# Second layer of a two-layer graph attention kernel: own rows loaded after their product, nine edge groups scaled by ScalarE, and the next exponent ahead of the activation

## The reference, cut to what matters

```
h = relu(layernorm(x));  x = x + attention0(h, input, adj, weight)
h = relu(layernorm(x)) @ W
e[m, n] = leaky_relu(h[m] . a_src + h[n] . a_dst)        where adj[m, n] > 0, else -1e9
att = softmax(e, axis=1);  att = where(att >= 1e-4, att, 0) * (valid entries of the row)
x = x + elu(h + att @ h)
```

## Time and profile before

| | |
|---|---|
| median of three runs | 630.43 us (630.30 to 631.12) |
| profiled execution | 629.07 us |
| its span, first to last instruction | 627.4 us |
| busy: TensorE, VectorE, ScalarE, GpSimd | 412.0, 462.9, 418.8, 300.1 us |
| VectorE's `take(1)` to `take(5)` start at | 551.06, 561.16, 572.24, 583.21, 594.18 us |
| last instruction of the second layer (VectorE) starts | 619.58 us |

### The profile page before, as it was taken

The page is one execution under the profiler, slowest core; times in us unless marked ns, Lnnn a source line. Parts: engine busy times, 40 slices in busy tenths (PEclk is TensorE's granted clock), DMA queues, the critical chain, the costliest instruction groups (busy, mean ns, idle before and its releaser), DMA issues.

```text
span 627.4 us, 9941 instructions
## 1 busy us (share of the span) xinstructions
PE 412.0 (66%) x3079; PEld 273.4 (44%) x3079; DVE 462.9 (74%) x2116; ACT 418.8 (67%) x460; POOL 300.1 (48%) x337
## 2 busy tenths in 40 slices
PE   2457476767877777786859677686756371268873
PEld 0112143443645455463635345363636361157653
DVE  0095268797979898997969799797986835279992
ACT  3567779889988989899879798988322030025451
POOL 6000851333315060607757563365777777777500
PEclk9655677997987979799969889799685675579998
DMA  8999999999999999999999999995122223235531
GB/s 322 414 419 422 419 405 408 409 406 412 403 414 380 370 401 392 403 388 404 396 402 384 395 387 399 390 376 188 53 69 64 60 74 103 54 71 154 141 103 54
DMA packets 37768, 186.80 MB, mean 298 GB/s; under 512 B 7888, under 2 KB 8144, under 8 KB 18896
## 3 DMA queue, kind: packets, MB, share of 16 engines
q1 hardware_dynamic: 28352, 166.75, 67.5%
q0 software_dynamic: 9216, 19.11, 10.6%
q10 hardware_dynamic: 144, 0.27, 0.1%
HBM read 179.73 MB, written 6.37 MB: 297 GB/s over the span
## 4 chain that ended last, share of the span: by engine, by line
DVE 36%; DMA 20%; ACT 12%; PE 11%; POOL 10%; issue 8%; SPq 2%; DVEq 0%; ACTq 0%
DMA arena<-in_adj 19%; ACT arena L892 8%; POOL arena L834 7%; PE K L1538 3%; DVE keys L1081 3%; POOL arena L826 2%; ACT R_all L921 2%; PE K L1783 2%; DVE G L1191 2%; DVE RTp L1485 1%; DVE RTp L1250 1%; DVE stats L1297 1%; ACT hx L901 1%; DVE cand L1110 1%; DVE cand L1098 1%
## 5 line engine op out<-in xcount | busy, mean ns | idle before, releaser
L892 ACT ACTIVATE arena<-arena,half_c 128x2048 fp8e4<-128x2048 int32 x144 | 284.2, 1999 | 45.5 <-DMA arena<-in_adj 40.2
L826 POOL DMA_INDIRECT X<-in_L_gnn_input,idx_all x132 | 125.4, 950 | 167.9 <-DVE idx_near L1162 130.4
L1538 PE MATMUL K<-arena,bits 128*128 128x512 fp8e4 x576 | 170.3, 436 | 16.8 <-ACT arena L892 16.7
L834 POOL DMA_INDIRECT arena<-table,idx_near x96 | 92.7, 965 | 36.8 <-issue 28.6
L1538 PEld LDWEIGHTS K<-arena,bits 128*128 128x128 bf16 x576 | 59.7, 109 | 91.0 <-ACT arena L892 25.9
L1081 DVE MAX8 keys<-K 128x8 int32<-128x128 f32 x192 | 42.4, 281 | 40.4 <-PE K L1538 40.3
L834 POOL DMA_INDIRECT E<-table,idx_near x48 | 46.0, 959 | 28.9 <-DMA table<-hs 14.5
L1536 PE MATMUL K<-key_add,key_one 128*128 128x512 bf16 x48 | 20.7, 430 | 45.2 <-ACT arena L892 23.4
L850 POOL TENSOR_TENSOR E<-E 128x3072 f32<-128x3072 f32 (+3 forms) x4 | 12.9, 3223 | 51.1 <-DMA E<-in_L_gnn_input 50.9
L1631 PE MATMUL W<-X,RTp 128*128 128x128 f32 x240 | 35.2, 285 | 1.2 <-ACT hs L937 0.8
L1550 PE MATMUL G<-g,R_all 128*128 128x128 bf16 x324 | 25.0, 226 | 16.1 <-DVE g L1213 13.5
(11 more groups left out here) (281 smaller groups left out, 962.2 us busy)
## 6 DMA issues: line engine op xcount, KB each, us to landing
arena<-in_adj SPq DMA_DIRECT2D x144, 1024.0 KB, 11.3
hs<-table SPq DMA_DIRECT2D x12, 262.0 KB, 2.8
E<-in_L_gnn_input SPq DMA_DIRECT2D x3, 1024.0 KB, 15.0
out_x<-x_all SPq DMA_DIRECT2D x12, 256.0 KB, 3.1
table<-hs SPq DMA_DIRECT2D x11, 262.0 KB, 7.8
x_all<-in_x SPq DMA_DIRECT2D x1, 2560.0 KB, 13.8
X<-in_L_gnn_input,idx_all POOLq DMA_INDIRECT x132, 5.6
arena<-table,idx_near POOLq DMA_INDIRECT x96, 2.7
```

The lines of the kernel that those rows point to most:

```text
L826: pool.indirect_dma_start(out=x_of(b)[:, e, :], out_offset=None, in_=inp, in_offset=bass.IndirectOffsetOnAxis(ap=idx_all[:, at:at + 1], ax ...
L834: pool.indirect_dma_start(out=E(g, t, 1)[:, 0, :], out_offset=None, in_=tables[g], in_offset=bass.IndirectOffsetOnAxis(ap=idx_near[:, t, g ...
L892: nc.scalar.activation(sign[:, load % SIGNS, :], ring[:, load % RING, :], ACT.Sign, bias=half_c[:], scale=1.0, saturate=False).then_inc(si ...
L1538: last = mm(bank_[:], bits[:, third * TB + j, :], sign[:, load % SIGNS, j * FOLD:(j + 1) * FOLD], start=False, stop=(third == G - 1 and j ...
```

## The change

Four edits, all in the second layer.

```
-    BY_ACT = 6
+    BY_ACT = 9
```

`own_r`, a new semaphore, is counted up by the matmul of `own_rows2(j)`, and SyncE waits for it in place of `att2_r`:

```
                 for j in range(T // B + 1):
                     if j + 2 < T // B:
-                        sp.wait_ge(att2_r, j + 1)
+                        sp.wait_ge(own_r, j + 1)
                         own(j + 2)
...
                     pe.wait_ge(h2_r[j % 2], 16 * sum(len(halves(k)) for k in range(j % 2, j + 1, 2)))
-                    mm(quads(att2[j % 4]), ident[:], h2[j % 2], start=True, stop=False)
+                    mm(quads(att2[j % 4]), ident[:], h2[j % 2], start=True, stop=False).then_inc(own_r, 1)
```

On ScalarE the exponent of group i comes before the odd block's activation:

```
                     if 0 <= i - 1 < NQ:
                         exponent2_of_edges(i - 1)
                         scale_last_edges(i - 1)
+                    if i < NQ:
+                        exponent2(i)
                     if 0 <= i - 2:
                         elu_parts(2 * (i - 2) + 1)
-                    if i < NQ:
-                        exponent2(i)
```

More of the change, by code:

```diff
@@ L625, in fast_path @@
         h2_r = [sem("h2_r0"), sem("h2_r1")]
-        take_early_r, take_r, rows2_r, cen2, ex2_r, pk_r, shares2_r, d2_r, exp2_e_r, RTp2_r, att2_r, src_r, neg_r, w_act_r, scaled_r, e_r, out_r, out_stored = (
-            sem(s) for s in ("take_early_r", "take_r", "rows2_r", "cen2", "ex2_r", "pk_r", "shares2_r", "d2_r", "exp2_e_r", "RTp2_r",
+        own_r, take_early_r, take_r, rows2_r, cen2, ex2_r, pk_r, shares2_r, d2_r, exp2_e_r, RTp2_r, att2_r, src_r, neg_r, w_act_r, scaled_r, e_r, out_r, out_stored = (
+            sem(s) for s in ("own_r", "take_early_r", "take_r", "rows2_r", "cen2", "ex2_r", "pk_r", "shares2_r", "d2_r", "exp2_e_r", "RTp2_r",
                              "att2_r", "src_r", "neg_r", "w_act_r", "scaled_r", "e_r", "out_r", "out_stored"))
```

## The result

The changed kernel took 625.81 us (median of seven runs, 623.43 to 627.41), the kernel before 630.30 in seven (629.63 to 631.31): ratio 0.9923, 95% interval 0.9904 to 0.9942, 4.5 us between medians and 3.7 to 6.1 by the interval. The profiled execution took 623.63 us, its span 622.1.

The account below looks back on a forecast made before the run. VectorE was taken to bound the four passes from take(2) to take(5), and a late own load the tail. Savings of 1.6 + 1.9 = 3.5 us took the median from 630.43 to 626.9 us, range 626.0 to 628.8.

Parts of the forecast that it names:

- Edit 1, VectorE's side: Second layer, VectorE's odd multiply: three groups instead of six take 0.54 us, saving 0.41 in each of four passes, 1.6 us.
- Edits 1 and 3, ScalarE's side: Second layer, ScalarE: after nine scalings, with the exponent in front, it still waits 0.65 us for the exponent's input; cost 0.
- Edit 2 and 4: Tail: last own load issued after block 9's own-rows product, not its attention product; ScalarE starts block 11 1.9 us earlier.
- The slower rival: Tail: TensorE's clock falls to 1.2 GHz for two products, costing 4.3 us more, 631.2 us; chance 0.05.
- Gathers come last: Second layer, takes from take(3) on: a late gather holds VectorE, giving 627.3 or 628.1 us; chance 0.12.

Follow-up runs that it names:

- e11_warm: Changed kernel with fourteen matmuls of 512 columns into an unused PSUM bank while TensorE waits in the pass of take(1); 625.43 us, ratio 0.9913 to the kernel before.
- the third trace: The changed kernel, unaltered, run and traced a third time; 628.20 us.
- edit 3: Part of the change to the kernel before: ScalarE's next exponent put in front of the odd block's activation; not measured by itself.
- e12_warm_by10: Changed kernel with ten groups by ScalarE in place of nine and fourteen extra TensorE matmuls in the pass of take(1); 624.77 us, ratio 0.9918 to the kernel before.
- e9_no_order: Changed kernel with the next exponent back behind the odd block's activation on ScalarE; 626.66 us, ratio 0.9934 to the kernel before.

## Why the prediction was off, step by step

**Edit 1, VectorE's side: right in size; one of the four passes is not VectorE's alone.** 0.54 us for three groups, 0.41 us a settled pass. The prediction's sentence that VectorE owned all four passes was read from one trace. In that one block 0's product ended at 560.81, before take(2) at 561.16. In most other traces it ends after take(2), and VectorE waits for TensorE. In the changed kernel's first trace:

```profile
DVE code_f L1459 <- PE SB L1766: 0.3, 1, 0.3
```

The pass of take(2) follows from this. With six groups it is 11.08 and 11.17 us in the two traces in which the product ended first, and 11.47 to 12.08 in the six in which it ended 0.06 to 0.65 us after take(2). In the changed kernel it is 10.56 where the product ended first (the third trace), and 11.20 and 11.84 where it ended 0.2 and 0.7 us late. So the saving is there in like traces, on top of a hold by TensorE of 0 to 0.9 us that differs from one execution to the next. The product takes 4.8 to 5.5 us here (the earlier trace rows has 4.84) and 2.7 in the later passes, since the granted clock is at its lower level for most of it. On average T13 goes from 21.54 us (six traces with six groups and a waiting TensorE) to 21.27 (three of the changed kernel); this 0.3 is smaller than the scatter within either group. e11_warm and e12_warm_by10, with the product ended before take(2), have passes of 10.64 and 10.54.

**Edits 1 and 3, ScalarE's side: right.** Nine scalings end 0.69 us before the exponent's input (0.65 forecast); without edit 3 the saving is gone in the trace (e9_no_order), as worked out.

**Edit 2 and 4: the mechanism right, the term mis-sized. This is the step that failed.** The prediction said "1.9 us" for the last own load. The product now starts on VectorE's multiply, as said, and against its own trace the early load gives 1.91. But the tail averages 26.47 us in the six traces, and 23.08 in the three of the changed kernel: 3.4 us in all, of which 0.4 is the multiply and 3.0 the load. The missing 1.1 are the clock's fall, some 1.6 us in four traces of six. The prediction left it out of the term, since it took one trace, without a fall, for the kernel. Counted from the other side, after the shorter passes, the load gives 1.8 us (24.9 to 23.08, no fall in either), so whether the 1.1 belongs to the load or to the shorter passes depends on which is made first; the whole change has it once.

**The slower rival had it backwards.** It priced a fall of TensorE's clock in the tail and called it unlikely, from one trace. The fall was already there, in the kernel before, and none of three traces of the changed kernel has it. The price was also too high: 4.3 us for two whole products at the lower level, where the falls that came cost 1.5 to 1.6 (and 3.5 / 2.15 is 1.63 products, not 1.65). A hint stood in the prediction, the median 1.36 us above the profiled execution. It is a weak one: the changed kernel's profiled execution lay 2.2 us below its median, and no trace of it has a fall.

**Gathers come last: no.** No take from take(3) on waits for one in the changed kernel, and with ten groups and the shortest passes still none.

**The end, in no step:** 7.85 us on average before and 7.56 changed, 0.3 us, not explained.

The sum of the averages: 0.3 (T13) + 0.85 (T35) + 3.4 + 0.3 = 4.85 us, against 4.5 and 4.6 between medians. It leaves out what lies ahead of take(1), and rests on six traces against three, so its agreement to a few tenths is in part luck. Where the wait lies sorts the traces with a fall from those without; why, is open, and what shortens the end is open too.

## What to carry to other kernels

A wait of TensorE on the path is priced by its length and by what the clock does to the work behind it; read the granted clock right behind every wait of 2 us that a change removes. One trace is one draw: take two more before a term is sized from it. Two parts of a change can each take out the same cost, and then their gains measured singly (4.7 and 3.5 us here) add up to more than the change gives (4.6). When work is moved onto a second engine inside a loop, the order on that engine decides whether anything is gained: here four waits of 0.34 us took back most of four savings of 0.41.

## What the runs showed of the hardware

The clock granted to TensorE can fall after a standstill of 2.2 to 2.4 us, and the same standstill (2.27 us) was also seen without a fall; it then stays low for three to four microseconds and costs 1.5 to 1.6 us (own product and 48 records: 7.99 to 8.11 us against 6.47). The standstills with a fall began 48.3 to 49.2 us after the clock had risen, those without 49.3 or 46.5 us after it; eight traces, not shown to be a rule. In the one trace with ten matmuls of 512 columns in the standstill the clock stayed at 1.00. VectorE's multiply took 1.75, 0.95, 0.54 and 0.41 us for 12, 6, 3 and 2 groups of 128 columns. What lies behind the last VectorE line was 7.81 to 8.06 us with six scalings a pass and 7.33 to 7.69 with nine or ten; eighteen idle instructions in ScalarE's program gave 7.60.
